# A cross-attention loop reordered: weighted sums of two key tiles in every second step, K and V units in pairs in the steps between, scores and maxima side by side

## The reference, cut to what matters

```python
x = x + L0_xattn(layernorm(x), ctx)     # K = ctx @ Wk.T, V = ctx @ Wv.T, softmax(q k / 4) v, @ Wo.T
x = x + L0_attn(layernorm(x))           # a small attention over heads
x = x + L0_ffn(layernorm(x))            # one expert of 8 per token
x = x + L1_xattn(layernorm(x), ctx)     # the same context, other weights, with biases
x = x + L1_attn(layernorm(x))           # a linear state scan, gelu, layernorm
x = x + L1_ffn(layernorm(x))            # two experts of 8 per token, gate, up, down
```

## Time and profile before

| | us |
|---|---|
| median of 3 runs | 1015.02 (1014.58 to 1016.22) |
| span of the profiled execution | 1012.9 |
| PE busy in it | 945.4 (93%) |
| DVE busy | 612.7 (60%) |
| ACT busy | 554.5 (55%) |
| POOL busy | 198.6 (20%) |

### The profile page before, as it was taken

The page is one execution under the profiler, slowest core; times in us unless marked ns, Lnnn a source line. Parts: engine busy times, 40 slices in busy tenths (PEclk is TensorE's granted clock), DMA queues, the critical chain, the costliest instruction groups (busy, mean ns, idle before and its releaser), DMA issues.

```text
span 1012.9 us, 35591 instructions
## 1 busy us (share of the span) xinstructions
PE 945.4 (93%) x15476; PEld 624.4 (62%) x15476; DVE 612.7 (60%) x1022; ACT 554.5 (55%) x1056; POOL 198.6 (20%) x233
## 2 busy tenths in 40 slices
PE   5589889999999999999999999998899999999998
PEld 2256555656666665666666666666678544445887
DVE  6456656577476656758666786785774774435322
ACT  5368676677767767665666656756634622212200
POOL 4212112121211112121121221213446200000000
PEclk9789999999999999999999999999799999999999
DMA  8677484553635443444344345324211432232100
GB/s 303 192 225 224 114 260 125 160 167 90 194 89 155 129 109 89 120 116 127 88 132 137 94 118 137 83 54 152 85 57 33 163 125 83 83 125 83 43 1 22
DMA packets 70829, 123.79 MB, mean 122 GB/s; under 512 B 34770, under 2 KB 46082, under 8 KB 67412
## 3 DMA queue, kind: packets, MB, share of 16 engines
q1 hardware_dynamic: 69812, 119.84, 39.8%
q0 software_dynamic: 576, 1.35, 0.4%
q10 hardware_dynamic: 288, 0.33, 0.1%
HBM read 64.81 MB, written 17.32 MB: 81 GB/s over the span
## 4 chain that ended last, share of the span: by engine, by line
PE 74%; DVE 10%; ACT 7%; issue 4%; SPq 3%; POOL 2%; DMA 1%; ACTq 0%; POOLq 0%; DVEq 0%
PE ps L717 72%; DVE mpart L1366 3%; ACT p L1122 3%; SPq L472 3%; DVE rinv L1383 2%; PE ps L856 1%; DVE cl L1341 1%; POOL xg L658 1%; ACT ch L1080 1%; PE ps L886 1%; DMA qbscratch<-qb 1%; ACT k L1096 1%; ACT kh L1097 1%; DVE oT L1386 1%; ACT L1122 0%
## 5 line engine op out<-in xcount | busy, mean ns | idle before, releaser
L1366 DVE TENSOR_REDUCE mpart<-ps 128x2 f32<-128x800 f32 (+1 forms) x256 | 252.3, 988 | 140.8 <-PE ps L717 139.6
L1122 ACT ACTIVATE p<-ps 128x512 f32<-128x512 f32 (+1 forms) x416 | 225.4, 595 | 175.2 <-PE ps L717 173.9
L646 POOL TENSOR_TENSOR kl<-k,kh 128x400 f16<-128x400 f32 (+1 forms) x128 | 118.2, 925 | 450.0 <-ACT kh L1097 450.0
L717 PE MATMUL ps<-p,v 128*17 128x64 f32 x6656 | 133.1, 223 | 2.1 <-issue 2.1
L717 PEld LDWEIGHTS ps<-p,v 128*17 128x17 f32 x6656 | 98.9, 98 | 39.4 <-issue 37.4
L717 PE MATMUL ps<-wvh,ch 128*128 128x256 f16 (+1 forms) x416 | 115.1, 277 | 0.0
L717 PE MATMUL ps<-wvl,ch 128*128 128x256 f16 (+1 forms) x416 | 114.2, 275 | 0.0
L717 PE MATMUL ps<-wvh,cl 128*128 128x256 f16 (+1 forms) x416 | 114.2, 274 | 0.0
L717 PE MATMUL ps<-xcl,wh 128*128 128x512 f16 (+2 forms) x384 | 112.9, 308 | 0.0
L717 PE MATMUL ps<-xch,wh 128*128 128x512 f16 (+2 forms) x384 | 112.8, 308 | 0.0
L717 PE MATMUL ps<-xch,wl 128*128 128x512 f16 (+2 forms) x384 | 112.8, 308 | 0.0
(11 more groups left out here) (208 smaller groups left out, 1447.8 us busy)
## 6 DMA issues: line engine op xcount, KB each, us to landing
ks<-kh SPq DMA_DIRECT2D x256, 100.1 KB
w<-in_wgu SPq DMA_DIRECT2D x16, 1024.0 KB, 4.8
ks<-kl SPq DMA_DIRECT2D x128, 100.1 KB
w<-in_wd SPq DMA_DIRECT2D x8, 1024.0 KB, 4.8
c32a<-in_ctxT SPq DMA_DIRECT2D x16, 400.5 KB, 4.7
cparts<-ch SPq DMA_DIRECT2D x8, 800.5 KB, 6.2
cparts<-cl SPq DMA_DIRECT2D x8, 800.5 KB, 8.6
c32a<-in_ctxT SPq DMA_DIRECT2D x12, 400.0 KB, 3.2
```

The costliest lines, as they stand in the source:

```text
L646: nc.gpsimd.tensor_tensor(kl[:, mt, k0:k0 + w], k32[:, ku % 2, 0:w], kh[:, mt, k0:k0 + w], ALU.subtract).then_inc(sem("klo_done"), 1)
L717: return nc.tensor.matmul(o, lhsT, rhs, start=start, stop=stop, skip_group_check=shared)
L1122: nc.scalar.activation(p32[0:n, step % PRING, BANK * side:BANK * side + BANK], ps[0:n, side, :], ACT.Exp, scale=DH ** -0.5).then_inc(sem(" ...
L1366: nc.vector.reduce_max(mpart[:, j0:j0 + 3:2, quarter], o.rearrange("p (b c) -> p b c", b=2)[:, :, 0:w], AX.X).then_inc(sem("max_done"), 1)
```

## The change

The table is written anew, `scores_first` goes away, and events get their own places in the table:

```diff
-STEP_UNITS = {0: ["V2", "S", "P0", "W"],
-              1: ["V3", "S", "P1", "W"],
-              2: ["V4", "P2", "V5", "S", "P3"],
-              3: ["W", "S", "P4"],
-              4: ["K4", "S", "P5", "W", "O"],
-              5: ["V6", "P6", "K5", "S", "P7", "W"],
-              6: ["K6", "S", "P8", "W"],
-              7: ["K7", "S", "P9", "W"],
-              8: ["V0", "P10", "V1", "S", "P11", "W"],
-              9: ["N0", "S", "P12", "W"],
-              10: ["N1", "S", "P13", "W"],
-              11: ["N2", "S", "P14", "W"],
-              12: ["S", "P15", "N3", "W", "T"]}
-WEIGH_AT = {0: (11,), 1: (12,), 3: (0, 1), **{k: (k - 2,) for k in range(4, KT)}}
-SUMS_STEP, DIVIDE_STEP = 2, 5
-SECOND_BANK = ("V3", "V5", "K4", "K5", "K7", "V1", "N1", "N3")
-CTX_STEPS = {3: 0, 5: 1, 7: 2, 9: 3}
+STEP_UNITS = {0: ["S", "P0", "W", "P1", "V2", "E"],
+              1: ["S", "P2", "E", "V3", "V4", "E"],
+              2: ["S", "P3", "W"],
+              3: ["S", "P4", "V5", "V6", "E"],
+              4: ["S", "P5", "W"],
+              5: ["S", "P6", "O", "K4", "K5", "E"],
+              6: ["S", "P7", "W"],
+              7: ["S", "P8", "E", "K6", "K7", "E"],
+              8: ["S", "P9", "W", "P10", "V0", "E"],
+              9: ["S", "P11", "E", "V1", "N0", "E"],
+              10: ["S", "P12", "W"],
+              11: ["S", "P13", "E", "N1", "P14", "N2", "E"],
+              12: ["S", "P15", "W", "T", "N3", "E"]}
+WEIGH_AT = {0: (12,), **{k: (k - 2, k - 1) for k in range(2, KT, 2)}}
+SUMS_AFTER, DIVIDE_AFTER = "P2", "K4"
+SECOND_BANK = ("V3", "V5", "K4", "K6", "V0", "N0", "N2")
+CTX_STEPS = {2: 0, 4: 1, 6: 2, 8: 3}
...
-def scores_first(units):
...
+def slots_of(k):
+
+    before = sum(STEP_UNITS[i].count("E") for i in range(k))
+    return iter(range(before, before + STEP_UNITS[k].count("E")))
...
 # on ACT:
-                    for name in scores_first(STEP_UNITS[k]):
+                    slots = slots_of(k)
+                    for name in STEP_UNITS[k]:
                         if name == "S":
                             exps(g, k)
+                        elif name == "E":
+                            for what, layer, t in events(g, next(slots)):
+                                event(what, layer, t)
                         elif name != "W" and has_unit(name, g):
                             after_unit(name, round_of(name, g))
                     if k in CTX_STEPS and g + 2 < B:
                         split_ctx(4 * (g + 2) + CTX_STEPS[k])
-                    for name, layer, t in events(g, k):
-                        event(name, layer, t)
...
 # on DVE:
-                        if k == SUMS_STEP and name == "P2" and g:
+                        if name == SUMS_AFTER and g:
                             take_sums(g - 1)
-                    if k == DIVIDE_STEP and g:
-                        divide(g - 1, 1)
+                        if name == DIVIDE_AFTER and g:
+                            divide(g - 1, 1)
```

More of the change, by code:

```diff
@@ L176, in has_unit @@
 def has_unit(name, g):
-    return name in ("S", "W") or 0 <= round_of(name, g) < G
+    return name in ("S", "W", "E") or 0 <= round_of(name, g) < G
 def turn_index(name, layer, t):
@@ L232, in users_before @@
         for k in range(KT):
+            slots = slots_of(k)
             for name in STEP_UNITS[k]:
+                if name == "E":
+                    for event in events(g, next(slots)):
+                        if event_read_by(*event):
+                            before[event] = last[3]
+                            last[3] = event_read_by(*event)
+                    continue
                 if name in ("S", "W") or not has_unit(name, g):
@@ L238, in users_before @@
                 last[at] = read_by(name, r)
[L239 to L242, removed]
     before["O", G - 1] = last[3]
@@ L601, in _ @@
                         store_parts(g + 2)
-                    for name, layer, t in events(g, k):
-                        event(name, layer, t)
[L604 to L607, removed]
+                    for slot_ in slots_of(k):
+                        for name, layer, t in events(g, slot_):
+                            event(name, layer, t)
+                            if name == "stage" and t + 2 < STAGE_JOBS:
+                                load_stage(t + 2)
+                            elif name == "stage" and t == STAGE_JOBS - 1:
+                                store_expert_bias()
                     if (g, k) == (2, 0):
@@ L978, in _ @@
                             scores(g, k)
-                        elif name == "W" and k > 1:
+                        elif name == "W" and k:
                             for kt in WEIGH_AT[k]:
@@ L984, in _ @@
                                 weigh(g - 1, kt)
+                        elif name == "E":
+                            for what, layer, t in events(g, next(slots)):
+                                event(what, layer, t)
                         else:
                             run_unit(name, round_of(name, g))
[L987 to L991, removed]
+            for kt in WEIGH_AT[0]:
+                weigh(G - 1, kt)
             parts, last_parts = iter(GATE_PARTS), iter(LAST_GATE_PARTS)
@@ L1598, in _ @@
                 for k in range(KT):
+                    slots = slots_of(k)
                     for name in STEP_UNITS[k]:
-                        if name not in ("S", "W") and has_unit(name, g):
+                        if name == "E":
+                            for what, layer, t in events(g, next(slots)):
+                                event(what, layer, t)
+                        elif name not in ("S", "W") and has_unit(name, g):
                             after_unit(name, round_of(name, g))
-                        if k == SUMS_STEP and name == "P2" and g:
+                        if name == SUMS_AFTER and g:
                             take_sums(g - 1)
-                    if k == DIVIDE_STEP and g:
-                        divide(g - 1, 1)
+                        if name == DIVIDE_AFTER and g:
+                            divide(g - 1, 1)
                     if k in CTX_STEPS and g + 2 < B:
                         split_ctx(4 * (g + 2) + CTX_STEPS[k])
-                    for name, layer, t in events(g, k):
-                        event(name, layer, t)
             take_sums(G - 1)
```

## The result

The change makes the kernel 8% slower: 1096.72 us (1094.93 to 1097.22) against 1015.59 us for the kernel before, measured beside it on one chip, a ratio of 1.0798 (1.0783 to 1.0813). The forecast of 1040 and its range to 1060 had the sign and missed the size by 57 us.

A forecast was written before the change was run, and what follows sets the result against it. PE's order of work was taken as the bound. Units +21.0, events +9.2, cover -5.4 made +24.8 on a 1012.9 us span: 1037.7; the median lies 2.1 above the span, so 1040, range 1010 to 1060.

The forecast's parts named there:

- Changes of shape, -15: On PE, 43 changes of matmul shape a round become 34, at 0.11 us each: 15 us saved over 15 rounds.
- The order of units, +21: A round without events: 3.19 us new waits, less 1.0 for shape changes and 0.79 for an old wait; +21.0 over 15 rounds.
- P1's wait: Step 0: P1 stands 0.84 us behind P0's start but needs 1.43 for the reduction; wait 0.59 a round.
- `T`'s: Step 12: `T` follows P15 at 1.94 us at the earliest, with only 1.29 of work between; wait 0.65 a round.
- the walk: Place-by-place timing of PE, ACT and DVE through a round without events; it found 3.19 us of new waits a round.
- step 7's `S`: Step 6's exponentials stand behind K5's copy on ACT, so the next step's scores wait 0.67 us a round.
- step 5's `S`: After short step 4, the next scores cannot start before 1.64 us, against 1.53 of PE work; wait 0.11 a round.
- The clause that exponentials first would be 17 us better: If ACT took exponentials ahead of copies, both 0.67 waits would be 0.11 and the sum 17 us lower.
- The 0.79 let go: Old wait of `P` for reductions behind `divide`, 0.79 us a round, taken to vanish in the new order.
- "Moved at no cost": K7's later copies delay the restack on SP's queue, but some 6 us of cover remain; no cost.
- "The other events I take as even": Events outside the priced places add work to ACT and DVE as well as cover on PE; net zero.
- The last rival, DVE's order: Reductions, `divide` and events queue on DVE: +55 us, 1070, from 1057 up; chance 0.10.

The follow-up runs named there:

- experiment 3: The changed kernel's order of units, but one slot of events at the end of each of the 13 steps: 1029.20 us.
- experiments 4 and 11: Kernel before with only the weighted sums regrouped: in pairs in steps 1, 3, 5, 7, 9, 11, 1016.63 us; with pairs in the light steps, 1014.51 us.
- experiment 2: Changed kernel, with ACT taking exponentials ahead of the one K, N or V copy directly before them: 1096.92 us.
- Experiments 1 and 6: First: changed kernel, query store ahead of step 8's restack on SP, 1070.38 us. Second: kernel before, only the query store moved behind that restack, 1039.31 us.
- experiment 5: Changed kernel with the query store ahead of the restack, and P reductions on DVE ahead of directly preceding events that only later events wait for: 1074.44 us.
- experiment 12: Changed kernel's order of units with one slot of events at each step's end, and in step 12 N3 ahead of `T`: 1041.05 us.

## Why the prediction was wrong

**Changes of shape, -15.** Right in kind: PE's work fell by 12.2 us in experiment 3 (the table of before has 44 changes, not 43, so ten a round go). In the change itself the page hides it, since work at a lower clock puts it back. But the term was booked as time, and in experiments 4 and 11, in the order of before, such turns came back as waits.

**The order of units, +21.** Near in its sum, 15.0 us, and right in several terms. In experiment 3, P1's wait comes to 10.1 us and `T`'s to 10.8, where the walk had 8.9 and 9.8. But step 7's `S` waits 2.2, not 10.1, since events cover it there, and step 5's `S` 8.2, not 1.7. Net, the walk had 36.0 us of new waits and the run has 26.5. Experiment 3 has its own places for the events, so this is the cost of the order with events spread out, not without any.

**The clause that exponentials first would be 17 us better.** Wrong for step 6, the half that experiment 2 reaches; step 10 was not tried. The row that the prediction showed and the rule of the strict queue agree, and the wait of 0.67 does go away in most rounds; but the walk did not follow the copy that then comes second. K7 waits for it, 0.54 in the row above, and nothing is gained.

**The 0.79 let go: too large a credit, 11.9 us.** It was one row taken for 15 rounds. In the kernel before, PE waits for reductions 13.7 us in all steps together, and the wait behind `divide` comes to 4.4, with 0.79 in the rounds 8 and 10 alone. Nor does it go away in the change: in the rounds 2 to 5 P7's reduction stands behind both halves of `divide` and P8 waits 0.81 (4.8 us with round 1). Round 3, DVE and PE:

```profile
213.17 0.98 DVE L1373 TENSOR_REDUCE mpart<-ps 128x2 f32<-128x800 f32 x1
...
214.21 0.35 PE L721 MATMUL ps<-kh,qbcur 64*128 64x401 f16 x2 [0.81 <-DVE mpart L1373]
```

P7 had started at 211.19. In experiment 3, with an event at the end of step 6, P8 does not wait.

**"Moved at no cost": the step that failed first, 26 us.** It priced the restack by who waits for the restack, and found 6 us of cover, rightly. It did not ask what stands behind 12 stores on SP's queue. The query store did, an event that the table moved from step 7 to step 8, and behind it DVE's `a_v`, the reduction and PE. Experiments 1 and 6 show it both ways.

**"The other events I take as even": the step that failed most, 41 us.** The prediction gave the event term 9.2 us less 5.4 of cover, and no more than 18, with DVE's order as the mechanism at two places of the rounds 3, 5, 7 and 9. There it was right: in experiment 1 P4 (behind `a_x`) waits 2.9 us in these rounds and P10 (behind `f_turn`) 5.9, where it had 4.0 and 5.2. The events that it took as even were not. P10 waits 8.1 us more in the even rounds, from round 2 on behind `out`, and the short steps 2 and 6 lost the events that had given PE work (step 7's `S`, P8, step 3's `S`). Nor had the sum a term for PE's clock: of the 42.8 us between the spans of the experiments 1 and 3, 35.0 are waits and 7.8 PE's busy time. The places are shown to cost this much; how it divides between reductions behind events, lost cover and the shorter way to the next event stays open.

The last rival, DVE's order, named the engine on which most of the loss shows, and one of its terms, the `divide` wait that stays, is there. Turning that order round gained nothing in experiment 5. That its 1070 is the time of experiment 1 is chance.

Together 15.0 + 41.2 + 26.3 = 82.5, against 81.1 between the medians of the first comparison; the kernel before was 1.4 us faster in the sets with the experiments.

No version here beats the kernel before; the two with pairs only come level with it.

## What to carry to other kernels

When a table of work is reordered, list for every engine and every DMA queue what now stands behind each moved item, not only who waits for the item itself. Price a small stage that moves by three things: whose work it now stands ahead of, what it covered at its old place, and how soon the next stage needs it. Changing who goes first on one engine may only choose where the wait shows. On an engine that waits now and then, time saved in its own work is not time saved, until the walk shows who releases it next.

## What the runs showed of the hardware

A stop of PE can cost more than its length. After 1.74 us of standing in experiment 12 the granted clock of the stretch was 0.85, and full-size matmuls started 0.21 to 0.22 apart (464.07 to 464.29) instead of the 0.11 of the kernel before: 1.2 instead of 2.4 GHz. After the 5.70 us stop of the change the stretch had 0.86. Ending those stops took 6.7 us off PE's busy time in experiment 1, beside 16.4 us of waits. Not every stop does it: after an equal one of 1.74 us that ended at 371.54 in experiment 12, the stretch shows 1.00:

```profile
370.00:375.00 5.00, 2.94 (x66) 2.31 (x67) 1.99 (x2) 2.51 (x5) 0.94 (x1) 1.00 0.33 79
```
